# Two graph networks on one core: a last product with nodes in rows, and messages kept in SBUF

## The reference

```python
h = relu(layernorm(x))
for m in range(3):                     # graph attention
    g = h @ Ws[m]                      # every node attends to its in-edges and to itself
    h = h + sigmoid(segment_sum(alpha[:, None] * g[src], dst) + bias[m])
x = x + h
h = relu(layernorm(x))
for l in range(3):                     # message passing, edge features e
    e = relu(concat(h[src], h[dst], e) @ We[l] + be[l])
    agg = segment_sum(e * norm[:, None], dst)
    h = relu(concat(h, agg) @ Wn[l] + bn[l])
return x + h
```

## Time and profile before

| | us |
|---|---|
| median of 3 runs | 6,092.61 (6,088.71 to 6,099.74) |
| the profiled execution | 6,093.98, span 6,092.1 |
| PE busy | 5,122.6 (84%) |
| DVE busy | 4,340.3 (71%) |
| ACT busy | 3,412.1 (56%) |
| GpSimd busy | 3,450.1 (57%) |

### The profile page before, as it was taken

The page is one execution under the profiler, slowest core; times in us unless marked ns, Lnnn a source line. Parts: engine busy times, 40 slices in busy tenths (PEclk is TensorE's granted clock), DMA queues, the critical chain, the costliest instruction groups (busy, mean ns, idle before and its releaser), DMA issues. The chain is left out here.

```text
span 6092.1 us, 100401 instructions
## 1 busy us (share of the span) xinstructions
PE 5122.6 (84%) x23996; PEld 3034.7 (50%) x23996; DVE 4340.3 (71%) x11924; ACT 3412.1 (56%) x7493; POOL 3450.1 (57%) x3533
## 2 busy tenths in 40 slices
PE   4999999999994768837773888799989997777785
PEld 2666666666651234424442444466656664333332
DVE  7888888888864799958885999555545544544443
ACT  4888888888874857736662677433323322222222
POOL 3544444444412557347755774477566654777777
PEclk9999999999997978868886999899999999999887
DMA  9999997777655867636664898676677774444442
GB/s 220 311 299 303 302 293 246 239 239 246 223 182 174 252 176 221 197 114 199 201 198 126 277 294 280 194 212 209 188 217 221 221 216 142 136 130 127 129 130 84
DMA packets 909508, 1274.03 MB, mean 209 GB/s; under 512 B 248502, under 2 KB 398967, under 8 KB 902579
## 3 DMA queue, kind: packets, MB, share of 16 engines
q1 hardware_dynamic: 696170, 1063.92, 53.0%
q0 software_dynamic: 112896, 202.19, 14.2%
q10 hardware_dynamic: 100016, 3.20, 1.2%
HBM read 623.49 MB, written 654.07 MB: 210 GB/s over the span
## 5 line engine op out<-in xcount | busy, mean ns | idle before, releaser
L1734 POOL DMA_INDIRECT n_xs<-table,look x1176 | 1116.1, 949 | 695.9 <-issue 318.2
L1439 POOL DMA_INDIRECT g_xs<-table,look x784 | 777.7, 992 | 454.5 <-issue 234.1
L1873 DVE TENSOR_TENSOR_SCAN n_dT<-n_km,n_dT,bank 128x512 f32<-128x512 uint8 x291 | 372.3, 1279 | 549.8 <-PE bank L1761 549.8
L626 POOL DMA_INDIRECT p_rows<-in_x_dram,dst_ix x392 | 389.1, 993 | 486.5 <-DMA raw_rows<-p_rows 259.0
L634 POOL DMA_INDIRECT table<-slot_pair,map_ix x392 | 396.0, 1010 | 457.0 <-ACT n_sg L742 249.2
L670 PE MATMUL bank<-n_xT,gat_w 128*128 128x512 f32 (+1 forms) x1176 | 542.8, 597 | 18.0 <-ACT n_xT L734 16.0
L689 PE MATMUL bank<-n_zT,wn 128*128 128x512 f32 (+1 forms) x1176 | 539.2, 594 | 6.6 <-ACT n_zT L734 6.6
L1746 POOL DMA_INDIRECT out_dram<-n_xn,n_row_of x392 | 385.6, 984 | 141.0 <-issue 118.2
L1838 ACT ACTIVATE n_eT<-bank,edge_b 128x512 f32<-128x512 f32 x294 | 201.7, 686 | 430.5 <-PE bank L1778 430.2
L1557 ACT ACTIVATE g_xw<-g_xs,g_cols 128x128 f32<-128x128 f32 x1176 | 370.6, 386 | 76.7 <-PE bank L1507 49.3
L1855 ACT ACTIVATE n_xn<-bank 128x512 f32<-128x512 f32 x98 | 58.5, 597 | 613.3 <-DMA out_dram<-n_xn,n_row_of 606.5
(11 more groups left out here) (275 smaller groups left out, 12462.6 us busy)
## 6 DMA issues: line engine op xcount, KB each, us to landing
table<-n_ro SPq DMA_DIRECT2D x768, 256.0 KB
g_gb<-decays SPq DMA_DIRECT2D x294, 256.0 KB
n_xd<-table SPq DMA_DIRECT2D x294, 256.0 KB
table<-g_xn SPq DMA_DIRECT2D x196, 256.0 KB, 4.2
g_xo<-table SPq DMA_DIRECT2D x196, 256.0 KB
edge_feats<-n_eT SPq DMA_DIRECT2D x196, 256.0 KB
table<-n_xn SPq DMA_DIRECT2D x196, 256.0 KB
n_ea<-edge_feats SPq DMA_DIRECT2D x196, 256.0 KB
```

The source lines that it names most:

```text
L626: q.indirect_dma_start(out=edge_rows[e % UX][:, u, :], out_offset=None, in_=x, in_offset=bass.IndirectOffsetOnAxis(ap=dst_ix[:, t:t + 1], ...
L1439: q.indirect_dma_start(out=xs[g % XR][:, u, :], out_offset=None, in_=tables[l], in_offset=bass.IndirectOffsetOnAxis(ap=src_ix[:, t:t + 1] ...
L1734: q.indirect_dma_start(out=xs.buffers[g % UE][:, u, :], out_offset=None, in_=tables[L], in_offset=bass.IndirectOffsetOnAxis(ap=look[:, t, ...
L1873: V.tensor_tensor_scan(in_order(dT[g][:, :]), kept(g), in_order(flat_banks[1]), 0.0 if begins(g) else carry(dT[g.before(1)]), ALU.mult, AL ...
```

## The change

In the node pass the third product of each chain swaps its operands. The nodes' feature-major tile is now held, 128 columns at a time, and the weights move, so the result has nodes in rows and needs no transpose back. Its bias no longer fits ACT's bias per partition. A bf16 matmul of three rows of ones with three bf16 parts of the bias opens the bank (`row_product`). In the d chain, ACT gates the rows and DVE adds them into n_mid, where group rows of stage 2 and n_xm were added before. In the z chain DVE takes bank 7 directly: ReLU and the add of n_mid in one instruction, so ACT's third ReLU goes. Bank 4 belongs to the d chain alone, bank 7 to the z chain. In passes 0 and 1, messages are written to a new SBUF tile n_mT, the norm bank is free once that is done, and PE's list has `weights` ahead of `nodes`.

```diff
-            xT = [ring(f"n_xT{m}_", 4 if 0 < m < 3 else 2) for m in range(4)]
+            xT = [ring(f"n_xT{m}_", 4 if m else 2) for m in range(3)]
-            zT = [ring(f"n_zT{m}_", 2) for m in range(4)]
+            zT = [ring(f"n_zT{m}_", 2) for m in range(3)]
...
+                    def row_product(bank, of, bias, weight, ready, freed, made):
+                        def fn(g):
+                            p = parts(g)
+                            pe.wait_ge(ready, g.count())
+                            after(pe, freed, g)
+                            T.matmul(bank[0:p, :, :], lhsT=ones3[:, 0:p], rhs=bias, start=True, stop=False,
+                                     skip_group_check=True)
+                            for k in range(U):
+                                last = T.matmul(bank[0:p, k, :], lhsT=of[g][:, k, 0:p], rhs=weight, start=False, stop=True,
+                                                skip_group_check=True)
+                            last.then_inc(made, 1)
+                        return fn
...
-                    unrolled(pe, GT, [(LAG_P[m], product(m)) for m in range(3)]
-                             + [(LAG_B[m], back(m)) for m in range(3)]
+                    unrolled(pe, GT, [(LAG_P[m], product(m)) for m in range(2)]
+                             + [(LAG_P[2], row_product(banks[4], xT[2], brow3[2][:, :, :], gat_w[:, 2, :],
+                                                       d_ad[1], d_sg[2], d_mm[2]))]
+                             + [(LAG_B[m], back(m)) for m in range(2)]
                              + [(6, enter(banks[0], h, done1, d_c0, d_t0))]
-                             + [(LAG_ZP[m], zproduct(m)) for m in range(3)]
-                             + [(LAG_ZB[m], zback(m)) for m in range(3)]
+                             + [(LAG_ZP[m], zproduct(m)) for m in range(2)]
+                             + [(LAG_ZP[2], row_product(banks[7], zT[2], brow7[2][0:3, :, :], wn[2][:, 0, :],
+                                                        c_re[1], c_rw[2], c_mm[2]))]
+                             + [(LAG_ZB[m], zback(m)) for m in range(2)]
...
+                    def gate_rows(g):
+                        p = parts(g)
+                        a.wait_ge(d_mm[2], g.count())
+                        after(a, d_rw[2], g, 2)
+                        S.activation(sg[2][g][0:p, :, :], banks[4][0:p, :, :], ACT.Sigmoid).then_inc(d_sg[2], 1)
...
-                             + [(LAG_ZP[m], relu(m)) for m in range(3)]
+                             + [(LAG_ZP[m], relu(m)) for m in range(2)]
...
-                            if m < 2:
-                                stored(g, r_st[m])
-                                V.tensor_copy(ro[m][g][0:p, :, :], banks[5 + m][0:p, :, :]).then_inc(d_rw[m], 1)
-                            else:
+                            stored(g, r_st[m])
+                            copied = V.tensor_copy(ro[m][g][0:p, :, :], banks[5 + m][0:p, :, :])
+                            if m == 1:
                                 after(v, done2, g, UN)
-                                V.tensor_tensor(group_of(of_macro(mid, g), g), banks[5 + m][0:p, :, :],
-                                                group_of(of_macro(xm, g), g), ALU.add).then_inc(d_rw[m], 1)
+                                copied = V.tensor_tensor(group_of(of_macro(mid, g), g), banks[5 + m][0:p, :, :],
+                                                         group_of(of_macro(xm, g), g), ALU.add)
+                            copied.then_inc(d_rw[m], 1)
...
+                    def gated_rows(g):
+                        of = group_of(of_macro(mid, g), g)
+                        v.wait_ge(d_sg[2], g.count())
+                        v.wait_ge(d_rw[1], g.count())
+                        V.tensor_tensor(of, of, sg[2][g][0:parts(g), :, :], ALU.add).then_inc(d_rw[2], 1)
...
+                        V.scalar_tensor_tensor(out=ro[4][g][0:p, :, :], in0=banks[7][0:p, :, :], scalar=0.0,
+                                               in1=group_of(of_macro(mid, g), g), op0=ALU.max, op1=ALU.add)\
+                         .then_inc(c_rw[2], 1)
-                    unrolled(v, GT, [(LAG_P[m] + 1, add(m)) for m in range(3)]
+                    unrolled(v, GT, [(LAG_P[m] + 1, add(m)) for m in range(2)] + [(LAG_ZB[2], out_rows_of)]
...
+                mT = None if last_layer else ring("mT", 2, (P, P * U))
...
-                            after(pe, total, g, NR)
+                            after(pe, total if last_layer else msg, g, NR)
...
-                            pipeline(pe, GE, [(4, enter), (7, nodes), (5, weights), (5, edges)], UE)
+                            pipeline(pe, GE, [(4, enter), (5, weights), (7, nodes), (5, edges)], UE)
...
-                            V.tensor_tensor(norm_of(g), norm_of(g), eT[g][:, :], ALU.mult).then_inc(msg, 1)
+                            V.tensor_tensor(messages_of(g), norm_of(g), eT[g][:, :], ALU.mult).then_inc(msg, 1)
```

More of the change, by code:

```diff
@@ L535, in build @@
         d_t0, d_c0, c_t0, c_c0 = (sem(k) for k in ("d_transposed", "d_copied", "c_transposed", "c_copied"))
-        d_mm, d_sg, d_ad, d_tr, d_rw = (sems(f"d_{k}", 3) for k in ("product", "gate", "added", "back", "rows"))
-        c_mm, c_re, c_tr, c_rw = (sems(f"c_{k}", 3) for k in ("product", "relu", "back", "rows"))
+        d_mm, d_sg, d_rw = (sems(f"d_{k}", 3) for k in ("product", "gate", "rows"))
+        d_ad, d_tr = (sems(f"d_{k}", 2) for k in ("added", "back"))
+        c_mm, c_rw = (sems(f"c_{k}", 3) for k in ("product", "rows"))
+        c_re, c_tr = (sems(f"c_{k}", 2) for k in ("relu", "back"))
         p_gx, p_rs = (sems(f"p_{k}", UX) for k in ("gathered", "rows_stored"))
@@ L749, in fn @@
                             a.wait_ge(c_mm[m], g.count())
-                            if m < 2:
-                                after(a, c_mm[m + 1], g, 2)
+                            after(a, c_mm[m + 1], g, 2)
                             after(a, c_tr[m], g, 2)
@@ L755, in relu @@
                         return fn
-                    unrolled(a, GT, [(LAG_P[m], gate(m)) for m in range(3)]
+                    unrolled(a, GT, [(LAG_P[m], gate(m)) for m in range(2)] + [(LAG_P[2], gate_rows)]
                              + [(6, enter(banks[0], xT[0], d_t0, d_c0, d_ad[0], 2)),
                                 (5, apply(0, done1, xm, h, h_st, d_t0))]
-                             + [(LAG_ZP[m], relu(m)) for m in range(3)]
+                             + [(LAG_ZP[m], relu(m)) for m in range(2)]
                              + [(22, enter(banks[1], zT[0], c_t0, c_c0, c_mm[0], 2)),
@@ L836, in fn @@
                             v.wait_ge(d_sg[m], g.count())
-                            after(v, d_tr[m], g, 4 if m < 2 else 2)
+                            after(v, d_tr[m], g, 4)
                             V.tensor_tensor(xT[m + 1][g][:, :, 0:p], xT[m][g][:, :, 0:p], sg[m][g][:, :, 0:p],
@@ L863, in fn, with out_rows_of @@
                             stored(g, r_st[2 + m])
[L864 to L870 removed]
+                            V.tensor_copy(ro[2 + m][g][0:p, :, :], banks[5 + m][0:p, :, :]).then_inc(c_rw[m], 1)
+                        return fn
+                    def out_rows_of(g):
+                        p = parts(g)
+                        v.wait_ge(c_mm[2], g.count())
+                        stored(g, r_st[4])
+                        V.scalar_tensor_tensor(out=ro[4][g][0:p, :, :], in0=banks[7][0:p, :, :], scalar=0.0,
+                                               in1=group_of(of_macro(mid, g), g), op0=ALU.max, op1=ALU.add)\
+                         .then_inc(c_rw[2], 1)
+                    unrolled(v, GT, [(LAG_P[m] + 1, add(m)) for m in range(2)] + [(LAG_ZB[2], out_rows_of)]
                              + [(1, newton), (0, stats(0, xm, x_ld))]
[L872 removed]
+                             + [(LAG_B[0], rows_of(0)), (1, newton), (LAG_B[1], rows_of(1)), (LAG_B[2], gated_rows)]
                              + [(16, stats(1, mid, None)), (LAG_ZB[0], zrows_of(0)), (1, newton), (LAG_ZB[1], zrows_of(1)),
[L874 removed]
+                                (1, shifts), (0, scales)], UN, (scales, newton, shifts))
         end_phase()
@@ L1674, in norm_of, with messages_of @@
                     return flat_banks[4 + g.c % NR]
+                def messages_of(g):
+                    return norm_of(g) if last_layer else mT[g][:, :]
                 with nc.Block() as block:
```

9 lines of the change are left out of this document (1 added, 8 removed).

## The result

The changed kernel takes 6,347.3 us (median of 4 runs, from 6,342.6 to 6,358.7), the kernel before, beside it, 6,094.4 us (4 runs). The ratio is 1.042, with a 95% interval from 1.040 to 1.044: slower by 253 us, where a gain of 35 us was forecast.

What follows compares the result with a forecast made beforehand. The prediction took PE to pace the node pass and message passes 0 and 1. It summed 6,094 + 25 - 60 = 6,059, or 6,058 us beside the median, with a range of 6,024 to 6,097 us.

Steps and rivals of the forecast that it cites:

- Node pass, the sum (+25): Node pass: the row product costs PE 0.12 us more, twice a step; 8.89 for 8.75 us over 180 steps, +25 us.
- the lower end's doubt: Node pass: perhaps no 0.10 us opens ahead of the bf16 bias behind a product; step 8.69 us, -11 us.
- The wait of every fourth step (none): Node pass: of PE's 0.39 us wait for DVE to free a bank every fourth step, almost nothing is left.
- (c): Node pass: DVE's late add makes PE wait 1.2 us every fourth step, 0.30 a step; 6,112 us, chance 9%.
- The margin: Node pass, fourth step: DVE as late as before, PE asks for its bank 0.35 us later, against a 0.39 us wait.
- Message passes (-60): Message passes 0 and 1: two bf16 matmuls side by side save 0.31 us a step, 192 steps, -60 us.
- its own 0.10: Passes 0 and 1: possible 0.10 us seam at the second adjacent bf16 matmul, leaving a gain of 0.21 a step.
- the estimate of 0.21: Passes 0 and 1: a bf16 product of 512 columns at a column a cycle, 2.4 GHz, takes 0.21 us.
- That GpSimd would be next: Pass 0: GpSimd's gathers, 4.99 us a group, come next after PE's new 5.10 us step; the gain barely fits.
- (a): Node pass has no seams, step 8.23 us, -94 us; message passes then gain nothing; 5,999 us, chance 5%.
- (b): The gain cancels: second bf16 matmul keeps its 0.10 us, every fourth step's wait stays; +3, 6,096 us, chance 17%.

Runs made afterwards that it cites:

- e3: The changed kernel with four buffers for ACT's row gate in place of two; 6,081.5 us, 0.998 of the kernel before.
- e4: The changed kernel, still two gate buffers, with DVE adding the gated rows one step earlier (lag 12, not 13); 6,085.9 us, 0.9985 of the kernel before.
- e8: The kernel before with only one wait added, the third d-chain gate on DVE's add into n_mid of two groups back; 6,338.7 us, ratio 1.039.
- e6: e3 with DVE's output operation at the end of the step in which its product is made; 6,089.6 us, 0.999 of the kernel before.
- e10: e7 with DVE's output operation directly behind the gated add, and four buffers and semaphores for output rows in place of two; 6,035.2 us, ratio 0.990.
- e7: e6 with both chains' bf16 bias matmuls side by side on PE, ahead of the eight fp32 ones; 6,132.8 us, 1.006 of the kernel before.
- e5: The changed kernel with the row gate last in ACT's list instead of third; 6,284.2 us, 1.031 of the kernel before.
- e12: The kernel before with only the messages of passes 0 and 1 in SBUF and the matching wait, PE's order unchanged; 6,091.5 us, ratio 0.9996.
- e11: The kernel before with only PE's order changed in passes 0 and 1, weights ahead of nodes; 6,034.5 us, ratio 0.990.
- e1: The kernel before with only the message edits of passes 0 and 1 (messages in SBUF, new wait, PE's order); 6,038.2 us, ratio 0.991.

## Why the prediction was wrong

**The step that failed.** It is this one: "ACT, busy 88%, loses the third ReLU. It is not the bound, so that is worth nothing." The prediction priced the row gate as work and did not price the wait that the change writes ahead of it, `after(a, d_rw[2], g, 2)`. Before, the reader of the third gate's slot was DVE's add at lag 12, one of the first three in its list: for a gate at lag 11 with a ring of two, the awaited add was done in the step before. Now the reader is the gated add at lag 13, the last of four operations that start behind PE's transposes, in the same step as the gate. That closes the circle shown above. Removed in two ways, it gives back 265.9 us (e3) and much the same (e4); put alone into the kernel before, it costs 244 us (e8). Each edit touches nothing but this wait, so the cause is shown. The size is not the same thing twice: e8's circle is looser (3.6 us in four steps, where the changed kernel loses 5.2 at the upper clock), and more of its loss is the lower clock. That ACT was busy 176 us of 200 said nothing about it: an engine that is no bound becomes a link as soon as its list stands still at a wait.

**Node pass, the sum (+25).** Right once the wait is gone. The row product measures 0.10 + 0.31 + 1.00 = 1.41 us (the two z products of 0.86 from 1002.38 end at 1004.10, and the next operation starts at 1005.51), as taken from the earlier trace rows; the seam opens behind a product too, which was the lower end's doubt. In e3 the pass is 38.6 us longer than before. The first n_zr transposes start 4.0 later (160.0 after 156.0) and the last n_h ones 30.5 (1752.5 after 1722.0), so some 26.5 belong to the steps with both chains, for 25 forecast. The 4 at the fill and the last 8 at the drain were not in the sum. In the drain PE waits for DVE's L901 (four times behind 1870 us, 3.3 to 8.4 us each), and L901 itself waits 78.3 us in all for output stores; before, PE waited three times for L865 and L867 (5.8 to 11.5), and L867 16.0 us for stores. Why the one costs 8 us more than the other was not tried alone. e6 excludes the place of the operation in DVE's list; e10, with four output slots, has an end 5 us shorter than the kernel before, which points to the two slots.

**The wait of every fourth step (none).** Right: e3's steps are 8.86 to 8.88, all alike, so rival (c) did not happen. The margin was as thin as reckoned: in e3's fourth step DVE's add (L878, from 1027.64) has emptied bank 6 at 1028.32, and PE wants it at 1028.44, 4.00 us behind the n_h transposes as forecast. In e7, where both row products stand ahead of the n_h transposes, PE wants it 1.41 us sooner and waits: L883 ends at 1013.26, and the transposes start at 1013.36 instead of 1012.90. The 0.92 us that PE waits later in that step is at bank 7, for the output operation that e6 had put last.

**Message passes (-60).** Right: 56.9 in the trace, 0.30 a step. "Whether the second bf16 matmul still shows its own 0.10" is answered: 0.23 and 0.22 from start to start against the estimate of 0.21. The Trainium skill ("TensorE: Matmul & The Clock Gate", "Step-by-step: what each phase is for") has PE pull weight loads ahead; the trace agrees between two matmuls of one type, bf16 now as well as fp32, and shows 0.10 us at every change of type. That GpSimd would be next did not decide: 5.11 is still above its 4.99.

**Rivals.** (a) is refuted by the seam in the node pass. (b) needed a seam at the second bf16 matmul, which is not there. (c) had the right sign and a late operation of DVE that others wait for, but the wrong waiter: it named PE, and it was ACT. It priced the wait at 0.30 us a step, 54 us in all, a fifth of the 265.9 that came.

**The sum of the miss.** 279.5 us in the node pass, 3.1 in the message passes, 0.9 elsewhere: 283.5 of 289.3. The other 5.7 are that the forecast was set 1 below the profiled time's sum and the profiled execution after stands 4.7 below its median.

## What to carry to other kernels

For each wait that a change writes or moves, find the step of the list in which the awaited work is done (the lags and the ring's depth give it), and whether that work depends, over the other engines, on what is queued behind the wait; if so, the step is the length of that circle, however idle the engines look. Two slots more (e3), or a reader one step earlier (e4), broke it here; moving the waiting instruction to the end of its list only closed another circle (e5). And look at the granted clock of the steps that got longer: idle time of PE brought the lower level with it in some of them, so that a loss can be larger than its wait. On TensorE, put matmuls of one type side by side: here each separate bf16 matmul costs 0.3 us in seams, and one moved entry gave 60 us of 6,094. The row form, with every repair, gave 6 us in its own pass.

## What the runs showed of the hardware

**Gathers wait for a scan that reads two tiles in SBUF.** With n_mT (the changed kernel, e12 and all with it) some gathers take up to 1.93 us instead of 0.94; without it (the kernel before, e8, e11) none takes over 1.00. GpSimd's and DVE's timelines, changed kernel:

```profile
4898.85 1.92 POOL L1772 DMA_INDIRECT n_xs<-table,look  x1 [0.30 <-issue]
```

```profile
4898.73 1.28 DVE L1924 TENSOR_TENSOR_SCAN n_aT<-n_km,n_aT,n_mT 128x512 f32<-128x512 uint8 x1
```

And in e12:

```profile
4205.61 1.35 POOL L1738 DMA_INDIRECT n_xs<-table,look  x1 [0.31 <-issue]
```

```profile
4204.93 1.28 DVE L1890 TENSOR_TENSOR_SCAN n_aT<-n_km,n_aT,n_mT 128x512 f32<-128x512 uint8 x1
```

The scans end at 4900.01 and 4206.21, the gathers 0.76 and 0.75 later, though they begin 1.16 and 0.60 ahead of the scan's end. In the changed kernel all 123 gathers begun between 0.1 and 1.0 us into such a scan end 0.75 to 0.76 behind it. In e12 48 gathers begin within its first 0.1 us; they take 0.94 as ever, and so do gathers that run already when the scan starts. The scan with one operand in PSUM does nothing of the kind. The Trainium skill, "SBUF — State Buffer", "SBUF: two separate sides", states this: a DVE operation with two SBUF inputs and a GpSimd operation that reads SBUF lock a shared pair of ports against each other. The trace agrees for the scan that comes first; for a gather that comes first it shows no delay, as no scan begun during a gather takes over 1.29 us. It cost nothing that can be told here (e12, and e1 beside e11), because the gathers had room; it takes part of the room that the prediction counted on.

**An activation without a bias column is shorter.** ACT's row gate takes 0.60 us for 128x512 (L769), the gate with a bias column 0.67 to 0.69 (L744 in e8: 0.69). The function is not the reason: in the kernel before the entry copy, without a bias, takes 0.60 on average and the ReLU with one 0.67. The prediction left the gate's price unchanged.
